# Splitting the sheaf stage's scans and doubling the message stage's output buffer in a graph network on one core

## The reference

```python
# layer 0, per edge, then summed and maximised over the edges of a node
m = jnp.concatenate([x[row], x[col], edge_attr], axis=1)
h = jnp.maximum(m @ W1 + b1, 0.0)
h = jnp.maximum(h @ W2 + b2, 0.0)
h = h @ W3 + b3
s = jax.ops.segment_sum(h, col, num_segments=n)
agg_max = jax.ops.segment_max(h, col, num_segments=n)
...
# layer 2 (sheaf), per edge; each F is 4x4, from a QR of six numbers of an MLP
Fve = _householder(_mlp(cat_ve, mlp1_w, mlp1_b, mlp2_w, mlp2_b))
Fue = _householder(_mlp(cat_ue, mlp1_w, mlp1_b, mlp2_w, mlp2_b))
msg = jnp.einsum('eka,ekb,ebh->eah', Fve, Fue, xjr)
msg = msg * (dis[col] * dis[row])[:, None, None]
agg = jax.ops.segment_sum(msg.reshape(-1, D * H), col, num_segments=n)
```

## Time and profile before

| | |
|---|---|
| median of 3 runs | 4694.56 us (4692.95 to 4698.24) |
| the profiled execution | 4687.18 us, its span 4685.4 us |
| PE busy | 2968.8 us, 63% |
| DVE busy | 3034.2 us, 65% |
| POOL busy | 1881.9 us, 40% |
| ACT busy | 1274.4 us, 27% |
| mean granted TensorE clock | 0.788 |

### The profile page before, as it was taken

One profiled execution on the slowest core, in us unless ns is written; L12 is line 12 of the kernel. 1 busy time (PEld: TensorE's weight loads), 2 busy tenths in 40 slices (PEclk: granted clock), 3 DMA queues, 4 the chain that ended last, 5 costly groups with the idle time before them and its releaser, 6 DMA issues. The chain is left out here.

```text
span 4685.4 us, 59450 instructions
## 1 busy us (share of the span) xinstructions
PE 2968.8 (63%) x19382; PEld 2193.7 (47%) x19382; DVE 3034.2 (65%) x4651; ACT 1274.4 (27%) x1892; POOL 1881.9 (40%) x1835
## 2 busy tenths in 40 slices
PE   1055556566642477779799699515766667673676
PEld 1034444344421254546556466315665666663455
DVE  9466676667623488756556466446677767774796
ACT  0011111111110277535345245101111111110484
POOL 4577777677762121100000000067777677642000
PEclk9966666666665699989899899657878788876698
DMA  5156666555630488534234144044454554541342
GB/s 178 33 136 152 155 154 150 145 149 149 153 83 13 184 333 325 202 132 157 77 144 160 60 152 149 1 91 86 100 120 100 106 118 93 114 85 26 111 167 73
DMA packets 738112, 599.57 MB, mean 128 GB/s; under 512 B 486055, under 2 KB 676612, under 8 KB 714476
## 3 DMA queue, kind: packets, MB, share of 16 engines
q1 hardware_dynamic: 462650, 389.91, 28.4%
q0 software_dynamic: 64032, 141.68, 10.5%
q10 hardware_dynamic: 211282, 66.03, 6.0%
HBM read 396.80 MB, written 200.61 MB: 128 GB/s over the span
## 5 line engine op out<-in xcount | busy, mean ns | idle before, releaser
L486 POOL DMA_INDIRECT ms_got_s<-table_src,ms_st_src x800 | 845.7, 1057 | 339.8 <-issue 332.1
L1553 POOL DMA_INDIRECT sh_got_s<-sheaf_src,sh_st_src x800 | 783.9, 980 | 301.9 <-issue 239.2
L1728 PE MATMUL sh_pin<-ident,sh_term 128*128 128x128 f32 x3200 | 465.5, 317 | 129.0 <-DVE sh_run L1663 114.5
L1728 PEld LDWEIGHTS sh_pin<-ident,sh_term 128*128 128x128 f32 x3200 | 455.8, 232 | 135.1 <-DVE sh_run L1663 120.2
L1047 DVE CUSTOM_DVE_ANT_0 c_xs<-c_pa,c_logs 128x1024 f32<-128x1024 f32 (+1 forms) x400 | 379.0, 967 | 187.9 <-PE c_pa L1154 109.5
L126 POOL DMA_INDIRECT spread<-dst_tab,first_idx x25 | 24.3, 971 | 1133.1 <-DVEq L100 1125.8
L991 PE MATMUL c_pa<-c_esT,c_v 128*64 128x128 f32 (+1 forms) x5000 | 399.8, 286 | 86.2 <-DVE c_esT L1061 61.7
L991 PEld LDWEIGHTS c_pa<-c_esT,c_v 128*64 128x64 f32 (+1 forms) x5000 | 278.0, 138 | 224.7 <-issue 119.3
L973 PE MATMUL c_pa<-ident,c_xs 128*128 128x128 f32 x2500 | 370.3, 287 | 0.0
L1154 PE MATMUL c_pa<-c_kT,c_q_st 64*128 64x512 f32 (+1 forms) x800 | 340.7, 546 | 43.4 <-DVE c_peaks L1047 27.7
L614 PEld LDWEIGHTS ms_pc<-ms_hot_l,ms_hot_x 128*125 128x125 bf16 x1408 | 211.5, 208 | 283.6 <-issue 263.5
(11 more groups left out here) (368 smaller groups left out, 5193.4 us busy)
## 6 DMA issues: line engine op xcount, KB each, us to landing
c_logs<-logs SPq DMA_DIRECT2D x75, 1562.5 KB, 6.5
prefix<-ms_sums SPq DMA_DIRECT2D x44, 1792.0 KB
logs<-c_logs SPq DMA_DIRECT2D x25, 1562.5 KB, 8.0
at_logs<-logs SPq DMA_DIRECT2D x25, 1562.5 KB
runs<-ms_out_t ACTq DMA_DIRECT2D x200, 128.0 KB
sh_cont<-cont SPq DMA_DIRECT2D x100, 256.0 KB
sums<-sh_out_t ACTq DMA_DIRECT2D x100, 256.0 KB
ms_seq<-in_dst_seq SPq DMA_DIRECT2D x200, 64.1 KB
```

Source lines behind the costliest of these rows:

```text
L486: pool.indirect_dma_start(got_s[u][:, i, q, :], None, dram["table_src"], bass.IndirectOffsetOnAxis(st_src[u][:, i, q:q + 1].bitcast(U32), ...
L1553: pool.indirect_dma_start(got_s[r][:, 4 * i + k, :], None, dram["sheaf_src"], bass.IndirectOffsetOnAxis(st_src[u][:, i, k:k + 1].bitcast(U ...
L1728: ins = pe.matmul(pin[j % 2][:, P * (i % 4):P * (i % 4) + P], term[:, 4 * i + 2 * k:4 * i + 2 * k + 2, :].rearrange("p t f -> p (t f)"), k ...
```

## The change

Five edits.

- Message stage: `out_t` becomes two buffers with a semaphore each. ACT waits for a buffer's DMAs only when it is to be written again, two blocks later.
- Message stage: the tile `h3` is gone. ACT writes the message with its bias back into the PSUM bank `p23`, from which both scans read.
- Both stages: POOL skips the 18 gathers whose tiles are padding alone, and the waits count accordingly. POOL's message loop is written out for its last three turns (six blocks).
- Sheaf stage: the four scans of a block are split. Scans 0 and 1 stand earlier, behind the first reciprocal of `messages` (`middle`), scans 2 and 3 stay behind `along`. PE turns pieces 2 and 3 ahead of all transposes back; of these, two stand before and two behind `hidden_and_entries`. ACT gets `sources` of the next block ahead of the copies of sums, and the DMAs come last in the block.
- Sheaf stage, start: `stage` for the first two blocks and the increments of `messaged` move to the head of DVE's stream, POOL waits for `zero` in place of `ready`, and two memsets clear only the part that no copy fills.

```diff
@@ -380,18 +380,18 @@
         h2 = ph.sb("h2", [P, BLK])
-        h3 = ph.sb("h3", [P, BLK])
         cont = [ph.sb(f"cont{u}", [P, BLK]) for u in range(2)]
...
         run_max = [ph.sb(f"run_max{u}", [P, BLK]) for u in range(2)]
-        out_t = ph.sb("out_t", [P, ST, 4, 2 * M])
+        out_t = [ph.sb(f"out_t{u}", [P, ST, 4, 2 * M]) for u in range(2)]
         p1, p23, pts, pd = (ph.ps(n, [P, BLK]) for n in ("p1", "p23", "pts", "pd"))
...
         multiplied, mm1, mm2, mm3, act1, act2, act3 = (ph.sem(n) for n in ("multiplied", "mm1", "mm2", "mm3", "act1", "act2", "act3"))
-        scanned, turned, masked, turned_out, out_st = (ph.sem(n) for n in ("scanned", "turned", "masked", "turned_out", "out_st"))
+        scanned, turned, masked, turned_out = (ph.sem(n) for n in ("scanned", "turned", "masked", "turned_out"))
+        out_st = [ph.sem(f"out_st{u}") for u in range(2)]
         dv, ds0, rows_turned, spread, added = (ph.sem(n) for n in ("dv", "ds0", "rows_turned", "spread", "added"))
@@ -407,6 +407,14 @@
         prefix = dram["prefix"][ND5:, :].rearrange("(i d) (h l) -> (d h) i l", d=ND5, l=LOW)
+        REAL = T2 - 3 * QT
+        def gathered(u, i, it):
+            if type(it) is not int:
+                return it * 64 + 64
+            return 16 * sum(4 - ((k * 2 + u) * ST + i >= REAL) for k in range(it + 1))
@@ -474,6 +482,8 @@
+            WHOLE = REAL // ST // 2
             def body(it):
@@ -483,11 +493,15 @@
                         for q in range(4):
+                            if q == 3 and type(it) is int and (it * 2 + u) * ST + i >= REAL:
+                                continue
                             pool.indirect_dma_start(
...
-            with pool.Fori(0, NB // 2) as it:
+            with pool.Fori(0, WHOLE) as it:
+                body(it)
+            for it in range(WHOLE, NB // 2):
                 body(it)
@@ -554,9 +568,9 @@
                 dve.wait_ge(act3, b + 1)
-                dve.tensor_tensor_scan(run_sum[u][:, :], cont[u][:, :], h3[:, :], run_sum[1 - u][:, BLK - 1:BLK],
+                dve.tensor_tensor_scan(run_sum[u][:, :], cont[u][:, :], p23[:, :], run_sum[1 - u][:, BLK - 1:BLK],
                                        ALU.mult, ALU.add)
-                dve.tensor_tensor_scan(run_max[u][:, :], gate[u][:, :], h3[:, :], run_max[1 - u][:, BLK - 1:BLK],
+                dve.tensor_tensor_scan(run_max[u][:, :], gate[u][:, :], p23[:, :], run_max[1 - u][:, BLK - 1:BLK],
                                        ALU.add, ALU.max).then_inc(scanned, 1)
@@ -632,7 +646,7 @@
                     for i in range(ST):
-                        pe.wait_ge(got[u][i], it * 64 + 64)
+                        pe.wait_ge(got[u][i], gathered(u, i, it))
                         ins = pe.matmul(p1[:, P * i:P * i + P], got_s[u][:, i, :, :].rearrange("p q m -> p (q m)"),
@@ -661,6 +675,8 @@
             act.sem_inc(turned_out, 1)
+            for u in range(2):
+                act.sem_inc(out_st[u], 64)
@@ -673,19 +689,21 @@
                     act.wait_ge(mm3, b + 1)
-                    act.activation(h3[:, :], p23[:, :], ACT.Identity, bias=b3[:, 0:1]).then_inc(act3, 1)
+                    act.activation(p23[:, :], p23[:, :], ACT.Identity, bias=b3[:, 0:1]).then_inc(act3, 1)
                     act.wait_ge(turned, b + 1)
+                    act.wait_ge(out_st[u], it * 64 + 64)
                     for of, lo in ((pts, 0), (p23, M)):
-                        ins = act.activation(out_t[:, :, :, lo:lo + M],
+                        ins = act.activation(out_t[u][:, :, :, lo:lo + M],
                                              of[:, :].rearrange("p (i q m) -> p i q m", i=ST, q=4), ACT.Copy)
...
                     for q in range(4):
-                        act.dma_start(quarter[q, b], out_t[:, :, q, :]).then_inc(out_st, 16)
-                    act.wait_ge(out_st, b * 64 + 64)
+                        act.dma_start(quarter[q, b], out_t[u][:, :, q, :]).then_inc(out_st[u], 16)
...
                 body(it)
+            for u in range(2):
+                act.wait_ge(out_st[u], 64 * (NB // 2) + 64)
             for u in range(2):
@@ -1489,6 +1507,14 @@
+        REAL = T2 - 3 * QT
+        def gathered(n):
+            if type(n) is not int:
+                return None
+            return 16 * sum(4 * SB - max(0, min(SB, m * SB - REAL)) for m in range(1, n + 1) if m % RING == n % RING)
         def is_block(n, *blocks):
@@ -1543,13 +1569,16 @@
                 u, r = c % 2, c % RING
+                n = number(c, it)
                 pool.reg_add(turn, turn, 1)
                 now = pool.snap(turn)
-                pool.wait_ge(ready, 1)
+                pool.wait_ge(zero, 1)
                 pool.wait_ge(staged, now)
...
                     for k in range(4):
+                        if k == 3 and is_block(n, *range(REAL // SB + 1, HB + 1)) and (n - 1) * SB + i >= REAL:
+                            continue
                         pool.indirect_dma_start(
@@ -1559,8 +1588,16 @@
             dve.memset(w2[:, :], 0.0).then_inc(zero, 1)
-            dve.memset(got_s[0][:, :, :], 0.0)
-            dve.memset(zin[:, :, :], 0.0)
+            def stage(b, u):
+                dve.tensor_copy(st_src[u][:, :, :].rearrange("p i k -> p k i"),
+                                keep["src"][:, :].rearrange("p (k t) -> p k t", k=4)[:, :, ds(b * SB, SB)]).then_inc(staged, 1)
+            stage(0, 1)
+            stage(1, 0)
+            dve.sem_inc(messaged, RING - 1)
+            dve.memset(got_s[0][:, NC:TB, :], 0.0)
+            dve.memset(zin[:, NC:TB, :], 0.0)
             dve.memset(basis[:, :, :, :, :], 0.0)
@@ -1576,11 +1613,6 @@
             dve.wait_ge(ready, 2)
-            dve.sem_inc(messaged, RING - 1)
-            def stage(b, u):
-                dve.tensor_copy(st_src[u][:, :, :].rearrange("p i k -> p k i"),
-                                keep["src"][:, :].rearrange("p (k t) -> p k t", k=4)[:, :, ds(b * SB, SB)]).then_inc(staged, 1)
@@ -1590,7 +1622,7 @@
-            def messages(n, r, s, between=lambda: None):
+            def messages(n, r, s, middle=lambda: None, between=lambda: None):
@@ -1612,6 +1644,7 @@
                 s.do(dve.reciprocal(inverse[:, :, :, 0], dots[:, :, :, 0]))
+                middle()
                 s.do(dve.tensor_tensor(ratio[:, :, :], dots[:, :, :, 1], inverse[:, :, :, 0], ALU.mult))
@@ -1656,9 +1687,10 @@
-            def scans(c, it):
+            def scans(c, it, pieces):
                 n, r = number(c, it), c % RING
-                for j, (k, h) in enumerate(PIECES):
+                for j in pieces:
+                    k, h = PIECES[j]
                     dve.wait_ge(turned, n * 4 + j - 3)
@@ -1666,22 +1698,26 @@
                 n, (r, turns) = number(c, it), ring(c, it)
-                dve.wait_ge(got[r], turns * 512 + 512)
+                dve.wait_ge(got[r], gathered(n) or turns * 512 + 512)
                 if not is_block(n, HB - 1, HB):
                     stage(n + 1, c % 2)
+                def middle():
+                    if not is_block(n, 1):
+                        scans(c - 1, it, (0, 1))
...
                     if not is_block(n, 1):
-                        scans(c - 1, it)
+                        scans(c - 1, it, (2, 3))
                 s = Steps(dve, dv, n * PER + LOOPS)
-                messages(n, r, s, between)
+                messages(n, r, s, middle, between)
                 assert s.n == PER
...
             loop(dve, body)
-            scans(TURN + 1, HB // TURN - 1)
+            scans(TURN + 1, HB // TURN - 1, (0, 1, 2, 3))
@@ -1730,30 +1766,38 @@
-            def sums_back(n):
-                for j, (k, h) in enumerate(PIECES):
+            def rest_to_scan(n):
+                for j in (2, 3):
+                    pe.wait_ge(scanned, n * 4 + j - 5)
+                    to_scan(j)
+            def sums_back(n, pieces):
+                for j in pieces:
+                    k, h = PIECES[j]
                     pe.wait_ge(scanned, n * 4 + j - 3)
-                    if j + 2 < len(PIECES):
-                        to_scan(j + 2)
                     pe.wait_ge(copied, n * 4 + j - 3)
...
             def body(c, it):
-                n = number(c, it)
+                n, last = number(c, it), number(c - 1, it)
                 if not is_block(n, HB):
...
                 if not is_block(n, 1):
-                    sums_back(number(c - 1, it))
+                    rest_to_scan(last)
+                    sums_back(last, (0, 1))
                 if not is_block(n, HB):
                     hidden_and_entries(number(c + 1, it), (c + 1) % 2)
+                if not is_block(n, 1):
+                    sums_back(last, (2, 3))
                 pe.wait_ge(messaged, n + RING)
...
             loop(pe, body)
-            sums_back(HB)
+            rest_to_scan(HB)
+            sums_back(HB, (0, 1, 2, 3))
@@ -1765,7 +1809,7 @@
                 r, turns = ring(c, it)
-                act.wait_ge(got[r], turns * 512 + 512)
```

(22 more changed lines are left out.)

2 lines of the change are left out of this document (removed).

## The result

The changed kernel takes 4453.79 us (median of 4 runs, 4452.92 to 4458.31), the one before 4695.58 us in the same series (4 runs, 4692.95 to 4698.24). The ratio is 0.9487, 95% interval 0.9471 to 0.9503: 242 us faster, where 230 were forecast. The profiled execution took 4453.98 us, its span is 4452.2 us; that of before was 4685.4, so the spans differ by 233.2 us. The profiled execution of before was 8 us faster than its median, which is why the two differences are not the same.

The account below looks back on a forecast made before the run. Message stage bound by a loop of waits through ACT, POOL close behind; sheaf stage by POOL once DVE's waits go. Message 125 plus sheaf 105 gives 230 us, the median from 4694.6 to 4465 us, range 4430 to 4535.

Parts of the forecast that it names:

- So with DVE's waits gone, POOL is what is left: Sheaf stage: POOL needs 41.0 us a block, DVE alone 32.9, so only 3.3 us a block can be gained.
- the third rival: POOL runs as freely as it can in both stages: message stage gains 137 us, 4449 us in total; chance 0.08.
- Two loops of 21.6 and 21.5 us side by side don't run at 21.6; I take 21.8: Message stage: the loop through `hin` and POOL's gathers together give 21.8 us a block, 101 us over 44 counting blocks.
- The check from POOL's side: Message stage: POOL's removable idle time, skipped gathers and shorter gathers, 93 + 22 + 22, allow at most 137 us.
- The 3.1 us a block: Message stage: ACT's wait for landed stores before the `hin` relu, 3.1 us a block, goes with the second output buffer.
- the rival: ACT stays the message loop's bound: store issue from 8.2 us on delays `hin`'s relu; at 9.4 us, 4509 us; chance 0.2.
- Price zero: Message stage: ACT writing the message into PSUM and both scans reading it there cost nothing more than with SBUF.
- The 22 us of relief on POOL: Message stage: with scans reading PSUM, one gather a block is 0.43 us shorter, 22 us over 50 blocks.
- POOL ends 79 us earlier: Sheaf stage: 56 us of POOL's idle time go, and 23 us with the skipped gathers.
- I take 57: Sheaf stage's end: 57 us from POOL's last gather to the last messages, 26 us less than before.
- DVE's wait of 3.67 us for the six numbers: Sheaf stage: DVE's 3.67 us wait per block, caused by ACT issuing stores before `sources`, was taken to go.
- The slower rival: Both stages: gathers stretch beside denser DVE work; 0.15 us each cancels the gain, 0.25 gives 4856 us; chance 0.04.

Follow-up runs that it names:

- e5: The changed kernel with the message written to the SBUF tile `h3` again, read by both scans: ratio 0.9526 to the kernel before.
- e6: The changed kernel with each DVE one-hot instruction made as two of half the size: ratio 0.9525 to the kernel before.
- e7: The changed kernel with each DVE one-hot instruction made as four of a quarter: ratio 0.9647 to the kernel before.
- e12: The changed kernel with halved one-hots, next block's rows turned before the first counts, and DVE's message-stage source-row copy two blocks ahead: 4433.15 us, ratio 0.9444.
- e2: The kernel before with only the second message output buffer: ratio 0.9774 to the kernel before.
- e3: The kernel before with only the message kept in its PSUM bank for both scans: ratio 0.9981 to the kernel before.
- e4: The kernel before with only the sheaf stage's edits, without its skipped gathers: ratio 0.9823 to the kernel before.
- e10: The changed kernel with PE turning the next block's first rows ahead of a block's first counts: ratio 0.9496 to the kernel before.

## Why the prediction was right

**The bound.** "So with DVE's waits gone, POOL is what is left", said of the sheaf stage, held there, and it held for the message stage too, where the prediction had the loop through `hin` at 21.6 us first and POOL right behind it at 21.5. POOL's idle time and the skips in both stages show it, and 13 us of gather time (e5) change the message stage by 11. The loop lies close behind, as e6, e7 and e12 show.

**The total is closer than its parts.** The message stage gave 14 us more than forecast, the sheaf stage 13 less. That the spans' 233 us lie so near the forecast 230 is luck in this sense; the mechanisms were right, the sizes off in opposite directions. The message stage came out as in the third rival (137 us, chance 0.08), the sheaf stage did not.

**Message stage, 138.8 us for 125.** The mechanism was right and the step "Two loops of 21.6 and 21.5 us side by side don't run at 21.6; I take 21.8" was mis-sized: the block is 21.2 us. The last six blocks gave 22 us where 19 + 5 were forecast, the 44 before them 117 in place of 101. Three things went into it. From `hin` to the sum scan I had 7.1 us; the block shown has 634.02 - 627.76 = 6.3, the mean is 6.6. The one-hot in it ended 3.6 us behind the start of `hin`, as forecast; what failed is the 3.44 us from the start of `counts(b, 3)` to the scan, taken over from the block before. Over the blocks between 600 and 1200 us the median of this stretch went from 3.2 to 2.5 us, and in the two blocks laid side by side TensorE's clock is at its lower level before and at its upper one after, a term that the prediction doesn't have. It came with the second output buffer: e2 alone has a granted clock of 0.73 over the 600 us and the eight matmuls at 0.88 us, e3 alone 0.64. POOL's 21.5 was too long as well: with the mean gather at 1.020 us it is 16 x 1.32 = 21.1. And the addition for two limits side by side was not needed. The check from POOL's side in the prediction, 137 us as "the most that it allows", was the better forecast. It was derived from sums over the whole stage, not from one block. Its 22 us of shorter gathers are 29 in the run (0.037 us x 782), 13 of them from the bank (e5) and the rest there without it (17 in e2).

**ACT's wait.** The 3.1 us a block were the landing, as said (e2). The issue of the stores did not rise above the 8.2 us that the rival needed, but `cont`'s issue went from 0.56 us to 0.9 to 2.6 us, and in the block shown the gate ends 0.3 us before the relu. The rival was close.

**The bank.** Price zero for ACT and for the scans holds: 0.66 and 1.28 us. The 22 us of relief on POOL were 13 of gather time (e5), 0.26 us a block and not 0.43; the stage's end moved by 11, the ratio by 18.

The Trainium skill's 62 cycles more for a VectorE operation from PSUM (VectorE: DVE Perf Modes, "The TRN2 errata") don't appear in these scans, 1.28 us from either; the measurement decides.

**Sheaf stage, 92.1 us for 105.** Two terms were too large. "POOL ends 79 us earlier": it was 71.3 (1081.6 us from the stage's start to its end, now 1010.3). The early start gave 11.5 us where 11 were forecast, and the waits went, but the mean gather rose from 0.980 to 0.986 us, 5 us over 782; e4 has 0.990. That DVE's two-input work lies denser would explain it and is not shown. POOL's idle time beyond 0.30 us a gather is 8.7 us, 5.3 of them before the first gather, where 6 were forecast. "I take 57" for POOL's end to the last messages: it is 60.0 us, and the scans and stores behind it took 30.1 in place of 28.0.

**A step that was right for less than it claimed.** I took DVE's wait of 3.67 us for the six numbers to go. It is still 3.74 us in the block shown from the middle of the stage. The wait for pieces 2 and 3 is gone as forecast; what is left of DVE's 106.5 us is for pieces 0 and 1. Nothing followed from it, since the same sum said that POOL is left anyway; the orders of PE, ACT and DVE are worth their result only up to POOL's 41 us.

**The slower rival** needed 0.15 us more for each gather. The message stage's mean fell by 0.037 us and the sheaf stage's rose by 0.006. The prediction's own sign of being wrong, "if a gather's mean rises above 1.05 and 0.98 us", did come up in the sheaf stage, at 0.986; it cost the 5 us above and not the mechanism.

## What to carry to other kernels

When an engine's idle time is small compared with the span, sum it over the whole stage first: as long as its own work stays the same, it caps the gain of every edit on the other engines, and here, with the work that goes added, it was the best forecast too. Edits that relieve an engine that waits measure as little alone and pay beside the edit that makes it the bound, so judge them in that company, or by the busy time in the trace: the skipped gathers gave 7 us alone, and 22.5 and 17 us in company. Once two loops are equally long, look for the small handover between them: moving a copy of 0.17 us took 13 us off POOL's idle time. And when an edit moves waits about, read TensorE's granted clock again in the stretch that sets the time. Here it helped the changed kernel by 0.6 us a block in one group of matmuls, and went the other way in e7 and e10.

## What the runs showed of the hardware

- A gather of POOL that starts beside a DVE instruction with two SBUF inputs is held until the end of that one instruction, then needs 0.82 us: 53 of 53 gathers over 0.99 us in 300 us of the changed kernel. Halving the instruction took the mean from 1.020 to 0.979 us. The Trainium skill, SBUF — State Buffer, "Who interferes with whom", says that a DVE instruction with two SBUF inputs contends with a GpSimd one that reads SBUF; the trace agrees. It shows besides that the hold lasts to the end of the instruction, and that a gather gets through between two such instructions back to back.
- A one-hot instruction of 0.68 us takes 0.74 us in two pieces and 0.89 in four; from its start to the next one's it is 0.59, 0.66 and 0.80 us. Eight one-hots a block at 0.21 us are 1.7 us. The stage lost 1.8 us a block with quarters, and TensorE's slower clock is in that too.
- The issue of the small `cont` transfer on ACT's queue takes 0.56 to 0.58 us in the kernel before, 4.5 us and more behind the four stores. In the changed kernel it comes 0.17 to 0.58 us behind them and takes 0.9 to 2.6 us. It isn't the nearness alone: in the blocks behind the counting ones, where the four stores take 2.1 us and not 5.4 to 7.2, it takes 0.56 us just as near to them.
- TensorE's granted clock differs between kernels that do the same matmuls: 0.66 in the message stage before (600 to 1200 us), 0.75 in the changed kernel, 0.70 in e7 and in e10. Eight matmuls of a count take 1.5 us at the lower level and 0.88 at the upper one.
